# Four graph layers on one core: one half of the one-hots moves to GpSimd, the edge bias and the moves of records to other phases

## The reference

```python
# L0 and L3: sums over the edges of a node
agg = segment_sum(h[src] * norm[:, None], dst)
# L1: maximum over the edges of a node
m = segment_max(leaky_relu(a_src[src] + a_dst[dst]), dst)
# L2: a bias of eight heads from the scalar weight of each edge
edge_bias = silu(edge_length @ We1.T + be1) @ We2.T + be2
attn = (q[row] . k[col]) / sqrt(HD) + edge_bias
```

## Time and profile before

| | before |
|---|---|
| median of 3 runs | 11864.83 us (11859.02 to 11871.73) |
| the profiled execution | 11860.36 us |
| its span in the trace | 11858.6 us |
| PE busy | 7046.0 us (59%) |
| DVE busy | 8063.0 us (68%) |
| ACT busy | 2369.6 us (20%) |
| POOL busy | 5619.7 us (47%) |
| L1269, `collect` in `cells_phase` | 4096 instructions, 343 ns in the mean |
| L1543, `maximum_phase` | 960 instructions, 1514 ns in the mean |

### The profile page before, as it was taken

The page is one execution under the profiler, slowest core; times in us unless marked ns, Lnnn a source line. Parts: engine busy times, 40 slices in busy tenths (PEclk is TensorE's granted clock), DMA queues, the critical chain, the costliest instruction groups (busy, mean ns, idle before and its releaser), DMA issues. The chain is left out here.

```text
span 11858.6 us, 183096 instructions
## 1 busy us (share of the span) xinstructions
PE 7046.0 (59%) x38485; PEld 5486.1 (46%) x38486; DVE 8063.0 (68%) x21893; ACT 2369.6 (20%) x6240; POOL 5619.7 (47%) x5516
## 2 busy tenths in 40 slices
PE   4899970066666637979400000677567777776398
PEld 4777760056666624545200000666455555555344
DVE  8999990168888892020599998888667777777601
ACT  0111110022222200010100000222145555555100
POOL 0677777622222200000077777777257777776000
PEclk9555555555555558989655555877679999999699
DMA  1000000056666656858366666888633333334176
GB/s 39 2 2 2 2 2 2 26 171 200 203 201 200 202 153 232 306 190 305 117 203 203 203 203 181 254 256 251 129 94 104 101 102 102 101 103 95 17 290 253
DMA packets 1113316, 1719.53 MB, mean 145 GB/s; under 512 B 250772, under 2 KB 814832, under 8 KB 1074864
## 3 DMA queue, kind: packets, MB, share of 16 engines
q1 hardware_dynamic: 565328, 1055.25, 26.5%
q0 software_dynamic: 204496, 358.11, 12.2%
q10 hardware_dynamic: 343056, 302.11, 8.6%
HBM read 1290.72 MB, written 424.01 MB: 145 GB/s over the span
## 5 line engine op out<-in xcount | busy, mean ns | idle before, releaser
L1458 POOL DMA_INDIRECT big<-tab_h,idx x1728 | 1959.9, 1134 | 2350.5 <-DMA tab_h<-asrc 1755.1
L2262 POOL DMA_INDIRECT big<-tab_kv,idx x1728 | 1674.6, 969 | 885.2 <-issue 468.8
L885 POOL DMA_INDIRECT by_src<-big,h x1568 | 1511.4, 964 | 495.6 <-issue 476.9
L1543 DVE SCALAR_TENSOR_TENSOR acc<-big,room,acc 128x1280 f32<-128x1280 f32 (+1 forms) x960 | 1378.8, 1514 | 21.2 <-DMA big<-cells 21.2
L1269 DVE SCALAR_TENSOR_TENSOR acc<-acc,h,banks 128x128 f32<-128x128 f32 x4094 | 1120.6, 343 | 262.2 <-DMA cells<-acc 260.7
L1807 DVE COPY acc<-banks 128x448 f32<-128x448 f32 x18 | 11.2, 625 | 1569.6 <-PE banks L1776 1568.0
L1776 PE MATMUL banks<-big,h 128*128 128x448 f32 x2744 | 1036.8, 541 | 17.4 <-DMA big<-cells 17.4
L934 POOL DMA_INDIRECT by_dst<-x,h x432 | 417.3, 966 | 1322.1 <-DVE room L398 724.3
L2337 PE MATMUL banks<-big,room 128*128 128x136 f32 x3456 | 635.4, 311 | 446.1 <-DVE acc L2434 444.1
L1666 PE MATMUL banks<-big 128*128 128x132 f32 x3456 | 683.0, 361 | 365.3 <-DVE acc L1691 362.4
L1527 PE MATMUL banks<-ident,acc 128*128 128x128 f32 x196 | 33.7, 348 | 1417.4 <-DVE acc L1543 1416.4
(11 more groups left out here) (476 smaller groups left out, 13244.4 us busy)
## 6 DMA issues: line engine op xcount, KB each, us to landing
big<-cells SPq DMA_DIRECT2D x262, 1568.0 KB, 6.3
cells<-acc SPq DMA_DIRECT2D x2049, 64.0 KB
cells<-acc ACTq DMA_DIRECT2D x2048, 64.0 KB
big<-cells ACTq DMA_DIRECT2D x196, 640.0 KB, 4.1
head_rows<-big SPq DMA_DIRECT2D x432, 264.0 KB, 2.1
big<-head_rows SPq DMA_DIRECT2D x216, 528.0 KB
acc<-w_rows SPq DMA_DIRECT2D x216, 512.0 KB
big<-loc_rows SPq DMA_DIRECT2D x216, 256.0 KB
```

What stands on the lines that cost most here:

```text
L885: pool.indirect_dma_start(k.by_src_dram, bass.IndirectOffsetOnAxis(k.pos[:, t:t + 1], axis=0), k.src_rec[:, t, :], None).then_inc(self.sca ...
L1458: pool.indirect_dma_start(k.stage[:, m % BODY, :], None, k.tab_h_dram, bass.IndirectOffsetOnAxis(k.idx[:, m:m + 1], axis=0)).then_inc(k.ga ...
L1543: ins = dve.scalar_tensor_tensor(mine, strip, k.small_asrc[:, src, h:h + 1], mine, ALU.min, ALU.max)
L2262: pool.indirect_dma_start(far[:, m % (G * RING), 0:2 * C], None, k.tab_kv_dram, bass.IndirectOffsetOnAxis(k.idx[:, m:m + 1], axis=0)).then ...
```

## The change

Five things change. In `cells_phase` POOL makes the one-hots of the sources, sixteen `tensor_scalar` of 128x128 for each half-turn that compare the ramp 0 to 127 with one column (`source`); the array is laid out column by column, and `k.cell_src` is in float32. DVE keeps the one-hots of the destinations, and PE waits for both (`made`, `sourced`). `k.cells` has room for two half-turns, and `stored` a semaphore for each half. The edge bias leaves `cells_phase`: SP, ACT, PE and DVE have only the cells there, and the spill of `k.big` in `prepare_phase` goes. It is computed in `maximum_phase` instead: SP fetches the weights between the stores of quads, ACT takes two units after each strip's `load` with six strips of delay (`LEAD`), with `neg` added as the bias of four small activations and stored to `bias_dram` at once, and PE adds `be2` by a matmul of one row. The folds there use six PSUM banks instead of eight. `Moves` leaves `cells_phase` and runs on POOL in the gather phases gcn1 (192 moves) and gcn2 (240 moves), without pacing.

```diff
@@ allocate
-    k.moved = [xx[:, m * CHUNK * UNIT * 4:(m + 1) * CHUNK * UNIT * 4].rearrange("p (j f) -> p j f", f=UNIT * 4)
+    k.moved = [room[:, m * CHUNK * UNIT * 4:(m + 1) * CHUNK * UNIT * 4].rearrange("p (j f) -> p j f", f=UNIT * 4)
...
-    k.cell_src = room[:, 0:Q // 2].bitcast(BF16)
+    k.cell_src = room[:, 0:Q]
...
+    k.cell_hot = [(spots[2 * m].rearrange("p (m c) -> p m c", c=P),
+                   spots[2 * m + 1].rearrange("p (o c i) -> p o c i", o=8, i=2)) for m in range(2)]
-    k.cells = k.acc[:, 4096:4096 + SUB * P].rearrange("p (r c) -> p r c", c=P)
+    k.cells = k.acc[:, 16 * P:16 * P + 2 * SUB * P].rearrange("p (c r x) -> p c r x", c=2, x=P)
@@ cells_phase, gpsimd
-            def pace(pool, t):
-                if t % 2 == 0:
-                    pool.wait_ge(made, t // 2 + 1)
-            moves.gpsimd(pool, pace)
+            def source(j, s):
+
+                at = j * (2 * SUB) + s * SUB
+                if j:
+                    pool.wait_ge(grown, j * 4 + s * 2 - 2)
+                for m in range(SUB):
+                    ins = pool.tensor_scalar(k.cell_hot[s][0][:, m, :], k.ramp[:, :],
+                                             k.cell_src[:, at + m:at + m + 1], None, ALU.is_equal)
+                ins.then_inc(sourced, 1)
+            pool.wait_ge(kept, 3 * len(rounds))
+            for j in range(CELL_TURNS):
+                source(j, 0)
+                source(j, 1)
@@ cells_phase, sync
-            with sp.Fori(0, both - 1) as j:
-                for s in range(2):
-                    store(sp, 0, j, s)
-                    sp.wait_ge(hidden, j * (2 * U) + (s + 1) * U)
-                    fetch(j + 1, s)
-            with sp.Fori(both - 1, CELL_TURNS) as j:
+            with sp.Fori(0, CELL_TURNS) as j:
                 for s in range(2):
                     store(sp, 0, j, s)
@@ cells_phase, tensor
                     pe.wait_ge(made, j * 2 + s + 1)
+                    pe.wait_ge(sourced, j * 2 + s + 1)
                     for b in range(2):
                         grow(j, s, b, first)
-                        if units:
-                            mix_step(j, s * U + b, first)
@@ cells_phase, vector
-                one_hots(dve, k, k.cell_hot[s][0], k.cell_src[:, at], P)
                 one_hots(dve, k, k.cell_hot[s][1], k.cell_dst[:, at], P).then_inc(made, 1)
...
-                            dve.wait_ge(stored[c][m // 4], j * 128 + s * 64)
+                            dve.wait_ge(stored[c][s][m // 4], j * 64)
...
-            dve.wait_ge(added, T // W)
-            lg = k.big[:, :].rearrange("p (t h) -> p t h", h=H2)
-            link(dve, dve.tensor_tensor(lg, lg, neg.unsqueeze(2).to_broadcast([P, T, H2]), ALU.add))
-            dve.tensor_tensor(lg, lg, k.be2[:, :].unsqueeze(1).to_broadcast([P, T, H2]), ALU.add)
@@ prepare_phase, sync
-            sp.dma_start(k.bias_dram, k.big[:, :]).then_inc(spilled, 16)
@@ maximum_phase
+    UNITS, FEW, LEAD = T // 4, T // 8, 6
...
+            def fetch(f):
+                if f >= 2:
+                    sp.wait_ge(hidden, 2 * (f - 1))
+                sp.dma_start(wide_w[:, f % 2, :], k.w_rows_dram[f * SIDE:(f + 1) * SIDE, :]
+                             .rearrange("t q -> (t q)").partition_broadcast(P)).then_inc(fetched[f % 2], 16)
+            fetch(0)
+            fetch(1)
             for z in range(AHEAD):
                 store_quad(k, sp, kept, z)
+                if z + 2 < FEW:
+                    fetch(z + 2)
...
+            def silu(n):
+
+                if n >= 2:
+                    act.wait_ge(mixed, n - 1)
+                act.activation(hid[:, n % 2, :], wide_w[:, n // 2 % 2, n % 2 * 4 * P:(n % 2 + 1) * 4 * P], ACT.Silu,
+                               bias=k.be1[:, 0:1], scale=k.we1[:, 0:1]).then_inc(hidden, 1)
+
+            def keep(n):
+
+                act.wait_ge(mixed, n + 1)
+                if n >= 4:
+                    act.wait_ge(stored[n % 4], n // 4 * 16)
+                for t in range(4):
+                    ins = act.activation(bias[:, n % 4, t * H2:(t + 1) * H2], mix[n % 2][:, t * H2:(t + 1) * H2],
+                                         ACT.Identity, bias=k.loc[:, 4 * n + t:4 * n + t + 1])
+                ins.then_inc(added, 1)
+                act.wait_ge(added, n + 1)
+                act.dma_start(k.bias_dram[:, n * 4 * H2:(n + 1) * 4 * H2], bias[:, n % 4, :]).then_inc(stored[n % 4], 16)
...
                 load(m)
+                f = m - LEAD
+                if 0 <= f < FEW:
+                    act.wait_ge(fetched[f % 2], 16 * (f // 2 + 1))
+                    silu(2 * f)
+                    silu(2 * f + 1)
+                if 1 <= f <= FEW:
+                    keep(2 * f - 2)
+                    keep(2 * f - 1)
...
+            def mix_unit(n):
+
+                pe.wait_ge(hidden, n + 1)
+                if n >= 2:
+                    pe.wait_ge(added, n - 1)
+                pe.matmul(mix[n % 2][:, 0:4 * H2], k.ones[0:1, :], level, start=True, stop=False, skip_group_check=True)
+                for t in range(4):
+                    ins = pe.matmul(mix[n % 2][:, t * H2:(t + 1) * H2], hid[:, n % 2, t * P:(t + 1) * P],
+                                    k.we2t[:, :], start=False, stop=True, skip_group_check=True)
+                ins.then_inc(mixed, 1)
+            pe.wait_ge(widened, 1)
+            ends = [min(UNITS, 2 * ((c + 1) * NB - LEAD)) for c in range(len(spans))]
+            for n in range(UNITS):
+                if n in ends:
+                    fold(ends.index(n))
+                mix_unit(n)
@@ gather_phase
+        if chunks:
+            moves = Moves(k, *chunks)
+
+            @block.gpsimd
+            def _(pool):
+                moves.gpsimd(pool)
@@ build
-        run(gather_phase, "gcn1", k.h, k.strips, k.total)
+        run(gather_phase, "gcn1", k.h, k.strips, k.total, (0, CHUNKS // 2))
...
-        run(gather_phase, "gcn2", k.h, k.strips, k.total)
+        run(gather_phase, "gcn2", k.h, k.strips, k.total, (CHUNKS // 2, CHUNKS))
```

More of the change, by code:

```diff
@@ L983, in cells_phase @@
     rowed = [k.sem(f"cut_rowed{r}") for r in range(4)]
-    fetched = [k.sem("bias_fetched0"), k.sem("bias_fetched1")]
-    hidden, mixed, added = (k.sem("bias_" + n) for n in ("hidden", "mixed", "added"))
-    gathered, brought, mapped, kept, addressed, made, grown, joined = (k.sem("cell_" + n) for n in (
-        "gathered", "brought", "mapped", "kept", "addressed", "made", "grown", "joined"))
+    gathered, mapped, kept, addressed, made, sourced, grown, joined = (k.sem("cell_" + n) for n in (
+        "gathered", "mapped", "kept", "addressed", "made", "sourced", "grown", "joined"))
     celled = [k.sem("cell_up"), k.sem("cell_down")]
-    stored = [[k.sem(f"cell_stored{c}{b}") for b in range(2)] for c in range(2)]
+    stored = [[[k.sem(f"cell_stored{c}{s}{b}") for b in range(2)] for s in range(2)] for c in range(2)]
     seam_stored = k.sem("cell_seam_stored")
@@ L1080, in _ @@
             for c in range(2):
-                for b in range(2):
-                    sp.wait_ge(stored[c][b], 4 * 16 * 2 * CELL_TURNS)
+                for s in range(2):
+                    for b in range(2):
+                        sp.wait_ge(stored[c][s][b], 4 * 16 * CELL_TURNS)
             sp.wait_ge(joined, 1)
@@ L1174, in _ @@
                         .then_inc(kept, 1)
[L1176 to L1208 removed]
+            act.wait_ge(addressed, 48)
+            with act.Fori(0, CELL_TURNS) as j:
+                for s in range(2):
+                    store(act, 1, j, s)
         @block.vector
@@ L1277, in _ @@
             collect(0, 0, True)
-            with dve.Fori(1, CELL_TURNS) as j:
+            hots(1, 0, False)
+            collect(0, 1, True)
+            hots(1, 1, False)
+            collect(1, 0, False)
+            with dve.Fori(2, CELL_TURNS) as j:
                 hots(j, 0, False)
@@ L1313, in _ @@
             sp.wait_ge(x_loaded, 32)
-            sp.wait_ge(spilled, 16)
         @block.tensor
@@ L1486, in maximum_phase @@
     steps = [(c, src) for c in range(len(spans)) for src in range(NB)]
+    hidden, mixed, added, widened = (k.sem("bias_" + s) for s in ("hidden", "mixed", "added", "widened"))
+    fetched = [k.sem("bias_fetched0"), k.sem("bias_fetched1")]
+    stored = [k.sem(f"bias_stored{r}") for r in range(4)]
+    UNITS, FEW, LEAD = T // 4, T // 8, 6
+    at = H1 * MAX_STRIP
+    wide_w = k.chunk_room[:, 0:2 * SIDE * P].rearrange("p (r c) -> p r c", r=2)
+    hid = k.acc[:, at:at + 8 * P].rearrange("p (r c) -> p r c", r=2)
+    at += 8 * P
+    bias = k.acc[:, at:at + 4 * 4 * H2].rearrange("p (r c) -> p r c", r=4)
+    at += 4 * 4 * H2
+    level = k.acc[0:1, at:at + 4 * H2]
+    mix = (k.psum[6], k.psum[7])
     with nc.Block() as block:
```

142 lines of the change are left out of this document (49 added, 93 removed).

## The result

The changed kernel takes 12440.6 us (median of 4 runs, 12432.35 to 12447.32). The kernel before, run beside it, took 11868.2 (11859.02 to 11871.73). The ratio is 1.0483, with a 95% interval from 1.0465 to 1.0501, so the change costs 572 us. The forecast was 11630 us, a gain.

A forecast was written before the change was run, and what follows sets the result against it. DVE was taken to bound the `cells_phase` loop, 83 to 98% busy, with POOL the bound after the change. Terms -212 + 4 - 23 - 12 + 8 = -235 us gave 11630 against 11864.8; own range 11400 to 11840, wider 11270 to 11980.

The forecast's parts named there:

- Half-turn, POOL: Loop of `cells_phase`: each of POOL's sixteen TENSOR_SCALAR takes 0.36 us, 5.76 us a half-turn.
- The bound above, 0.46: Upper estimate for one POOL TENSOR_SCALAR: 0.395 us for 48 columns, 0.46 with 80 more at 0.84 ns.
- POOL is too slow: Rival, loop of `cells_phase`: above 0.417 us an instruction the change loses; at 0.46, 8.50 us a half-turn, 12040 us; chance 0.14.
- POOL also stops under L1269: Rival, loop of `cells_phase`: a half-turn would be over 10 us and the time above 12400; chance 0.04.
- The two together: Loop of `cells_phase`: POOL stands for DVE's 1.14 us of one-hots, 6.90 us a half-turn, 1766 against 1978 us, -212.
- Half-turn, DVE: Loop of `cells_phase`: one of two one-hots and the store waits go, leaving a floor of 5.55 us, 1421 for 256.
- Start: Start of the `cells_phase` loop: the first grow waits for POOL's sixteen instead of two one-hots, +4 us.
- end of the phase: End of `cells_phase`: L1290 and L1291, 14.6 us each, go; the phase ends near 4438 instead of 4461, -23 us.
- prepare phase: End of `prepare_phase`: without the bias spill the load of `x` is late, the phase ends near 4482, -12 us.
- moves: Gather phases: 192 and 240 moves take 242 and 302 us under PE's more than 500; 0, at worst +10 us.
- Bias in `maximum_phase`: `maximum_phase`: ACT's 5.3 us a strip fits under DVE's 5.85; startup and folds add +8 us, from 0 to +60.
- The forecast's rival for this phase: ACT or the DMA engines bound `maximum_phase`: 11630 becomes about 11800; a loss there of 60 us or more, chance 0.09.

The follow-up runs named there:

- the pairs: The changed kernel with eight POOL TENSOR_SCALAR of 256 columns a half-turn in place of sixteen of 128: 11808.6 us in one execution.
- the twice-made one-hots: The changed kernel with a second one-hots of the destinations by DVE into a spare place each half-turn: 12621.4 us in one execution.
- The alternated order: Kernel with six of sixteen source columns on POOL, ACT's order in `maximum_phase` changed to keep, Silu, keep, Silu: 11380.1 us, 0.9576 of the kernel before.
- The increments: Increments of an unused semaphore at the start of DVE's list in `prepare_phase`; in the kernel before, 8 took 11948.0 us and 128 took 11893.3.
- 32 increments: The kernel before with 32 increments of an unused semaphore at the start of DVE's list in `prepare_phase`: 11746.4 us in one execution.
- the 96 increments: 96 unused semaphore increments on DVE in `prepare_phase`, in the kernel with both one-hots on DVE and ACT's keep before Silu: 11666.9 us against 11653.9.
- The eight-column, alternated kernel: Both one-hots on DVE, then eight of sixteen source columns on POOL, ACT's order keep, Silu, keep, Silu in `maximum_phase`: 11349.4 us in one execution.

## Why the prediction was wrong, point by point

**Half-turn, POOL: the step that failed.** "I take a fixed part of 0.25 and 128 x 0.84 = 0.11, together 0.36 us". The fixed part was right (0.26 to 0.28). The price per column was taken from an IOTA, which reads nothing; it measured 2.5 ns, three times that, so one instruction costs 0.577 and not 0.36 us. This term alone is 256 x 16 x 0.217 = 889 us. Whether the tensor that is read, its types or the operation makes a column of TENSOR_SCALAR three times as dear as one of IOTA, no run separates; the compared column does not. The bound above, 0.46, used the same 0.84 ns for its last 80 columns and was no bound. The sentence in brackets that a price per column of the TENSOR_SCALAR would lie "far above" named the true case: with the fixed 0.23 of the whole IOTA, the 0.395 us of the earlier trace rows give (0.395 - 0.23) / 48 = 3.4 ns a column, 0.67 us. That belonged in the range. The real value lay between the two readings of one row.

**The rivals.** "POOL is too slow", given a chance of 0.14, came true beyond its price of 8.50 us a half-turn. The forecast's estimate from the Trainium skill (GPSIMD Engine Reference, Performance versus the Vector engine), 9.6 us a half-turn by the price for two inputs, came near the 10.13 measured, though this operation has one. For one input, this operation's case, the Trainium skill (the same page, Engine selection) has "roughly line-rate", and the 2.5 ns a column measured do not agree. "POOL also stops under L1269" gave over 10 us too, and would have been the wrong reading of the right time: the sixteen instructions keep 0.597 us under L1216, and the pairs, the same elements in half the instructions, took 7.69 us.

**The two together.** Right, and the twice-made one-hots confirmed it: POOL stands while DVE reads two tensors of SBUF. The price was 0.93 instead of 1.14 us a half-turn. The forecast's own sum with the measured instruction and this price is 256 x (9.23 + 0.93) = 2601 us; the loop took 2594.0. The mechanism was right, and the size of one term was wrong.

**Half-turn, DVE.** The floor of 5.55 us was not reached: in every kernel in which DVE made one array only, POOL was the bound. With both arrays it was 6.64 us, with six columns moved 6.25, with eight 6.12, so its arithmetic (0.071 us a column) holds, and the store waits went as said.

**Start, end of the phase, prepare phase, moves.** The first grow was forecast at +4, and the loop starts 9.7 us later. For the end and `prepare_phase` the forecast was -23 and -12; they measured -40.9 together. The moves cost 1.2 us in the gathers. These terms were right to within 6 us.

**Bias in `maximum_phase`.** Forecast +8, measured +102.6, outside its own 0 to 60. ACT's work fits, as computed: it is busy 46%. "PE, with ten small matmuls a strip, was busy 20 of 1100 us there" looked at what PE did before and priced nothing of what it would do: two units are 2 x 2.36 = 4.7 us at the 1.2 GHz level (granted clock 0.50 to 0.51). With 4.7 us on PE in every 5.85, any stretch of over 1.1 us in which PE must wait for ACT decides, and the order Silu, Silu, keep, keep has one of 1.62. The alternated order, with the same work, takes 1441.4. So the cause is the dependence, not a unit. The forecast's rival for this phase named ACT's own work and the DMA engines, and neither bound it. Its remark that the fetches behind the quads only couple POOL and DVE was too mild: the long gather above passed through that coupling and cost 15 to 20 us in four of the kernels.

**`attend_phase`, -119.5 us.** Not forecast: no edit touches it. The increments show that the kernel before loses this time to instruction fetches. That the changed kernel gains it by the shift of DVE's code is inferred from its packets (23) and its length (2221.2 against 2222.8 us with 32 increments); it was not undone there, since the 96 increments did not hit the place.

## What to carry to other kernels

Before work moves to an engine that has no row of the same operation and size, price the elements and the fixed part separately, take the price of an element only from a row of the same operation that reads what the new one reads, and let the range hold a reading of the nearest row in which all of it is a price per element. A share of the work may pay where the whole does not: all sixteen columns on POOL lost 894 us, eight won 132 (1699.6 to 1567.8). Two engines that hand units to each other are priced as a chain: the time of a round is one engine's work plus whatever the other does in one piece while the first can't go on. And when a phase that no edit touches changes its length, look at the packets of the instruction queue and at "issue" in front of the loop's first instruction before looking for a cause in the data.

## What the runs showed of the hardware that was not expected

A loop's body can be fetched anew in each turn, for 118 to 186 us in 53 turns, depending on its place within 128 instructions: 282 to 285 packets of 8 KB against 27. The Trainium skill (Runtime: NRT & Kernel Launch, Instruction fetch mechanics) gives the room for instructions as 512 for most engines, refilled in blocks of 256, with the cost mostly hidden. In q14 of this trace a packet has 8192 bytes (376 with 3.08 MB; the other instruction queue, q8, has 60 of 16384), the loss returns after 128 instructions, and it isn't hidden. The 4.9 packets more in each turn would fit a body that fills the room in one place and reaches into one block more in another, so that all are fetched again. That is an argument: the trace doesn't record every wait of the body, so its length isn't known here, and no run varied it.

A gather of POOL can last 42 to 46 us beside DVE's unbroken instructions with two SBUF tensors, and end 0.8 us after their first hole begins. One wait of DVE for a strip, 15 to 20 us long, follows from it.

The eight-column, alternated kernel is the fastest here: 11349.4 us in one execution. The six-column, alternated one, measured four times, takes 0.9576 of the kernel before.
